# Tower of a small language model on one core: scores that add onto the ones left in their slot

## The chip, the cores and the metric

The kernel runs on one core of a Trainium2 chip. The metric is the device time of one execution in microseconds (us). Matmuls run on TensorE (PE in the rows; PEld is its weight load), elementwise work on VectorE (DVE), ScalarE (ACT) and GpSimd (POOL); SyncE (SP) issues most DMAs. TensorE writes its results to PSUM, which has eight banks of 512 fp32 columns; SBUF is the memory from which the engines read their operands.

## The reference

Two sequences of 1024 token ids go through an embedding with a short grouped convolution and a relu, then attention, then a mixture of experts with a fixed assignment of tokens. Nearly all of the time is attention:

```python
dots = jnp.einsum('bhqd,bhkd->bhqk', q, k) * scale      # 8 heads of 64, 1024 queries, 1024 keys
attn = jax.nn.softmax(dots, axis=-1)
out = jnp.einsum('bhqk,bhkd->bhqd', attn, v)
...
out = jnp.einsum('bne,ce->bnc', out, Wo)
```

Everything is fp32, and q and k are scaled so that softmax needs the maximum of each row.

## The kernel before

**Steps.** Eight steps (s, `STEPS`): two sequences, four pairs of heads each. A step has the queries in two halves of 512 and the keys in eight chunks of 128 (kc): 16 units. A unit is a PSUM slot of two banks, 128 keys by 2 x 512 queries (one bank for each head of the pair).

**A unit** (`scores`, L556). The operands are split in a rounded part and a rest, so that three products of reduced-precision matmuls, k_round q_round, k_round q_rest and k_rest q_round, give nearly fp32. Each product is a pair of matmuls, one for each head, with 64 rows and 512 columns, that run side by side. A fourth pair subtracts the maximum of each query (`minus_rows` times `max_rows_of`). ScalarE then takes exp of the slot into a tile of `probs` (L761), GpSimd adds the tiles for the denominators (L1160), and TensorE multiplies them with v into `acc_o` (L583), which has one bank for each half of the queries. In 44 of the 128 units (`FILLED`) the fourth pair is left out: ScalarE writes minus the maxima into the slot beforehand (`fill`, L813), from a plane that a DMA spreads over all partitions (`max_planes`), and the three products add onto it.

**Maxima.** A step ahead, TensorE makes rough scores of the next step with queries on the partitions (L509), VectorE reduces them (L961), joins the halves (L970) after each four chunks, and SP moves them by eight small DMAs to rows (`max_rows_of`, L386), a half (four chunks) at a time. Two maximum items stand in each part, as long as there are any; `AHEAD` is how many of them the prologue does.

**Order.** A step has eight parts of two units each. Every engine walks the same list of items and does its own share of each (`part_items`, L93), in program order: a maximum, two units, a maximum, then in part 0 k and q of the next step (twelve matmuls, L497; ScalarE copies the rounded parts, L770, VectorE subtracts for the rests, L956), in part 3 the denominators of the step before (L594), in step 7 the parts of the feed-forward (Wo, transposes, xa), a fill, and last the values (`pv`) of the two units of the part before. Every item that needs PSUM takes the next of three slots in turn (`n % SLOTS`), and TensorE waits until the item three places before has been read out (`release`).

**After the steps** the experts run in eight duos (L628, L639, L647). The prologue ahead of them makes the embedding, the normalised x, v (L476, through the two banks of `acc_o`), k and q of step 0, and the first maxima.

## Time and profile before

| | |
|---|---|
| Median of 3 runs | 408.73 us (408.3 to 408.97) |
| Profiled execution, its own time | 409.11 us |
| Its span | 407.2 us |
| TensorE matmuls busy | 395.0 us (97%) |
| VectorE busy | 224.5 us (55%) |
| ScalarE busy | 254.7 us (63%) |
| GpSimd busy | 292.7 us (72%) |
| Granted TensorE clock | 0.999 |

Times within the trace count from the start of the span. A matmul's length in the trace includes the time until its results have drained, so matmuls in a row overlap: what one costs is the distance from start to start.

### The profile page before, as it was taken

Reading aid. Unit: us, or ns where it says so; the run is one execution under the profiler, and the core shown is the slowest. Engines: PE = TensorE matmul, PEld = TensorE weight load, DVE = VectorE, ACT = ScalarE, POOL = GpSimd, SP = SyncE. Lnnn points to the kernel's source line nnn. Section 1 sums busy time; section 2 is a strip of 40 time slices with the busy share of each in tenths; the row PEclk is TensorE's granted clock in tenths of the full one; section 3 lists DMA queues with packets and bytes.
Section 4 is the critical chain, followed back from the end, with each engine's and each line's share of the span. In section 5 each row is a group of like instructions: output and inputs, shape, how many; then the busy total and the mean of one; then the engine's idle time right before and its main releaser. Section 6 shows DMA issues by size and latency. Waiting matters only on the chain.

```text
span 407.2 us, 6494 instructions
## 1 busy us (share of the span) xinstructions
PE 395.0 (97%) x2518; PEld 238.1 (58%) x2518; DVE 224.5 (55%) x304; ACT 254.7 (63%) x347; POOL 292.7 (72%) x145
## 2 busy tenths in 40 slices
PE   8898999999999999999999999999999989999996
PEld 8765554454555445544645555464558535489995
DVE  1798765565656555656665565657563700564322
ACT  1556566676667575767676575858573596436763
POOL 3062088969899989999998999899989487900011
PEclk9999999999999999999999999999999999999999
DMA  7000101011220121012103222240125014000001
GB/s 247 2 1 0 54 0 54 6 47 26 82 52 2 54 54 52 3 54 54 52 2 105 48 110 54 54 150 7 57 52 157 0 55 155 2 1 14 15 26 53
DMA packets 28507, 20.49 MB, mean 50 GB/s; under 512 B 21276, under 2 KB 23708, under 8 KB 28476
## 3 DMA queue, kind: packets, MB, share of 16 engines
q1 hardware_dynamic: 27900, 19.09, 17.3%
q10 hardware_dynamic: 576, 0.98, 0.7%
q8 instruction: 20, 0.33, 0.3%
q14 instruction: 11, 0.09, 0.1%
HBM read 18.77 MB, written 1.17 MB: 49 GB/s over the span
## 4 chain that ended last, share of the span: by engine, by line
PE 88%; DVE 4%; ACT 2%; DMA 2%; SPq 1%; issue 1%; POOL 0%; ACTq 0%; POOLq 0%
PE acc_o L583 27%; PE slot L571 24%; PE slot L509 9%; PE slot L497 6%; PE slot L518 4%; PE acc_o L639 4%; PE slot L628 4%; PE acc_o L476 2%; PE acc_o L436 2%; DVE half_maxes L961 2%; PE slot L594 2%; DMA max_plane<-rows_scratch 1%; SPq L386 1%; PE slot L451 1%; PE slot L534 1%; PE acc_o L451 1%
## 5 line engine op out<-in xcount | busy, mean ns | idle before, releaser
L961 DVE TENSOR_REDUCE half_maxes<-slot 128x2 f32<-128x1024 f32 x128 | 156.3, 1225 | 98.1 <-PE slot L509 97.9
L761 ACT ACTIVATE probs<-slot 128x1024 f32<-128x1024 f32 x128 | 124.7, 1024 | 82.2 <-PE slot L571 82.2
L583 PE MATMUL acc_o<-probs,v_all 128*64 128x512 f32 x512 | 123.7, 604 | 0.0
L1160 POOL TENSOR_TENSOR sums<-sums,probs 128x1024 f32<-128x1024 f32 x31 | 74.0, 2387 | 2.4 <-ACT probs L761 2.3
L1160 POOL TENSOR_TENSOR odd_sum<-odd_sum,probs 128x1024 f32<-128x1024 f32 x31 | 74.5, 2404 | 0.0
L1160 POOL TENSOR_TENSOR sums<-probs 128x1024 f32<-128x1024 f32 x16 | 37.9, 2368 | 44.0 <-ACT probs L761 44.0
L583 PEld LDWEIGHTS acc_o<-probs,v_all 128*64 128x64 f32 x512 | 31.2, 136 | 59.0 <-issue 39.7
L509 PE MATMUL slot<-k_round,q_round 64*128 64x512 f32 x256 | 56.9, 447 | 1.6 <-DVE half_maxes L961 1.3
L509 PEld LDWEIGHTS slot<-k_round,q_round 64*128 64x128 f32 x256 | 23.6, 183 | 57.0 <-issue 46.3
L571 PE MATMUL slot<-q_round,k_round 64*128 64x512 f32 x256 | 51.8, 400 | 1.7 <-ACT slot L819 0.8
L571 PE MATMUL slot<-q_round,k_rest 64*128 64x512 f32 x256 | 50.6, 390 | 0.0
L571 PE MATMUL slot<-q_rest,k_round 64*128 64x512 f32 x256 | 50.5, 389 | 0.0
L819 ACT ACTIVATE slot<-max_plane 128x1024 f32<-128x1024 f32 x44 | 45.2, 1028 | 2.8 <-DMA max_plane<-rows_scratch 1.7
L1166 POOL TENSOR_TENSOR sums<-sums,odd_sum 128x1024 f32<-128x1024 f32 x16 | 38.0, 2377 | 1.3
L1160 POOL TENSOR_TENSOR odd_sum<-probs 128x1024 f32<-128x1024 f32 x16 | 38.3, 2394 | 0.0
L1188 POOL TENSOR_TENSOR probs<-probs,residual 128x256 f32<-128x256 f32 x7 | 5.1, 726 | 43.2 <-ACT probs L870 43.2
L571 PE MATMUL slot<-max_rows_of,minus_rows 64*128 64x512 f32 x168 | 33.3, 389 | 0.0
L571 PEld LDWEIGHTS slot<-q_round,k_round 64*128 64x128 f32 x256 | 24.0, 184 | 11.3 <-issue 3.2
L571 PEld LDWEIGHTS slot<-q_round,k_rest 64*128 64x128 f32 x256 | 24.3, 184 | 5.4
L571 PEld LDWEIGHTS slot<-q_rest,k_round 64*128 64x128 f32 x256 | 24.2, 185 | 3.6
L863 ACT ACTIVATE probs<-slot,small 128x128 f32<-128x128 f32 x64 | 17.4, 383 | 11.4 <-PE slot L628 11.4
L571 PEld LDWEIGHTS slot<-max_rows_of,minus_rows 64*128 64x128 f32 x168 | 16.0, 184 | 3.3
(114 smaller groups left out, 423.1 us busy)
## 6 DMA issues: line engine op xcount, KB each, us to landing
max_plane<-rows_scratch SPq DMA_DIRECT2D x16, 512.0 KB, 3.6
inv_sb<-inv_scratch SPq DMA_DIRECT2D x14, 256.0 KB, 3.9
max_rows_of<-maxes SPq DMA_DIRECT2D x128, 0.5 KB, 2.0
v_all<-in_fc SPq DMA_DIRECT2D x4, 512.0 KB, 5.9
fc_late<-in_fc SPq DMA_DIRECT2D x4, 512.0 KB, 5.6
residual<-in_x SPq DMA_DIRECT2D x2, 512.0 KB, 5.9
out_h<-probs SPq DMA_DIRECT2D x8, 128.0 KB, 1.8
v_all<-in_w ACTq DMA_DIRECT2D x3, 256.0 KB, 7.4
```

The source lines that it names most:

```text
L497: last = pe.matmul(slot[:, half * BANK:(half + 1) * BANK], ws[:, w, v % PAIRS, :], xs[:, cols], start=(i == 0), stop=(i == 2))
L509: last = pe.matmul(slot[:, h * BANK:(h + 1) * BANK], q_round[p][head_rows(h), qc * CHUNK:(qc + 1) * CHUNK], k_round[p][head_rows(h), half ...
L518: last = pe.matmul(slot[:, j * C:(j + 1) * C], attn_out[:, b * PAIRS + r, j * CHUNK:(j + 1) * CHUNK], woT[:, r, :], start=(r == 0), stop=( ...
L571: last = pe.matmul(slot[:, h * BANK:(h + 1) * BANK], stationary, qs[head_rows(h), cols], start=(i == 0 and not ahead), stop=(i == len(term ...
L583: last = pe.matmul(acc_o[head_rows(h), cols], v_all[:, s, kc, head_rows(h)], probs[unit(s, kc, half) % TILES][:, h, :], start=(kc == 0), s ...
L628: last = pe.matmul(slot[:, i, r], expert(e)[:, 0, r, :], xaT[:, toks], start=True, stop=True)
L761: act.activation(probs[u % TILES][:, :, :].rearrange("p h n -> p (h n)"), slot[:, :], ACT.Exp, scale=SCALE).then_inc(exped, 1)
L819: act.activation(slots[n % SLOTS][:, :], max_planes[half][:, :], ACT.Copy, scale=-1.0).then_inc(filled_in, 1)
L863: act.activation(hidT[d % 2][:, i, r, :], slot[:, i, r], ACT.Gelu, bias=fc1_b_col[:, e * HC + r:e * HC + r + 1]).then_inc(hid_made, 1)
L961: dve.reduce_max(half_maxes[:, :, qc, keys], slot[:, :].rearrange("p (h n) -> p h n", h=2), AX.X).then_inc(maxed, 1)
L1160: pool.tensor_tensor(chain[:, :, :], first[:, :, :], probs[kc][:, :, :], ALU.add).then_inc(own, 1)
L1166: pool.tensor_tensor(even[:, :, :], even[:, :, :], odd_sum[:, :, :], ALU.add).then_inc(own, 1)
```

## The change

Within a half, the chunks of keys are taken in the order 0, 4, 1, 5, 2, 6, 3, 7 (`chunk_of`). Units with even kc use one slot, odd ones the other. Only the first unit in each slot (kc 0 and 1) computes its scores whole, with the pair for the maxima. Each later one adds (key chunk minus the chunk before it) times q onto the scores that are still in the slot, and has three pairs. `fill`, the planes and their DMAs are gone.

The third slot is for maxima alone (and in step 7 for transposes, xa and the last denominators). `acc_o`'s second bank becomes the place of k, q, the denominators and Wo; both halves' outputs go to its first bank in turn, but for the last half. k and q of the next step come in four pieces of 512 columns, between the first maximum and the units of parts 0, 1, 2 and 4. For each piece of k, ScalarE copies the first three chunks (`k_before`) and the rounded piece, and VectorE makes the rounded differences, their rests and the rest of the first chunk. `AHEAD` is 10 instead of 12, and the last four tiles of v come behind an earlier maximum.

The lists of items and places:

```diff
-AHEAD = 12
+AHEAD = 10
...
-                 ("max", *MAXES[7]): (8, 9, 10, 11), ("max", *MAXES[10]): (12, 13, 14, 15)}
+                 ("max", *MAXES[7]): (8, 9, 10, 11), ("max", *MAXES[9]): (12, 13, 14, 15)}
...
-FFN_ITEMS = {(STEPS - 1, 0): [("wo",)], (STEPS - 1, 3): [("nt",)], (STEPS - 1, 5): [("xa",)], (STEPS - 1, 6): [("last den", 0)]}
-
-
-PREFILLED = (2, 4, 6)
-UNFILLED = ((0, 2, 0), (STEPS - 1, 4, 0), (STEPS - 1, 4, 1))
+FFN_ITEMS = {(STEPS - 1, 0): [("wo", 1)], (STEPS - 1, 3): [("nt",)], (STEPS - 1, 5): [("xa",)], (STEPS - 1, 6): [("last den", 0)]}
+
+
+def chunk_of(kc):
+
+    return kc // 2 + kc % 2 * (KCH // 2)
...
-def beside_values(s, part):
-
-    items = []
-    if part == 0 and s + 1 < STEPS:
-        items += [("k", s + 1), ("q", s + 1)]
+def side_item(s, part):
+
+    if s == STEPS - 1 and part == 0:
+        return [("wo", 0)]
+    if s + 1 < STEPS and part in (0, 1, 2, 4):
+        return [{0: ("k", s + 1, 0), 1: ("k", s + 1, 1), 2: ("q", s + 1, 0), 4: ("q", s + 1, 1)}[part]]
+    return []
+
+
+def part_items(s, part):
+
+    maxes = [("max", *m) for m in MAXES[AHEAD + 2 * (s * PARTS + part):][:2]]
+    items = maxes[:1] + side_item(s, part)
+    items += [("exp", *u) for u in units_of(s, part)] + maxes[1:]
     if part == 3 and s > 0:
         items.append(("den", s - 1))
-    return items + FFN_ITEMS.get((s, part), [])
-
-
-def part_items(s, part):
-
-    maxes = [("max", *m) for m in MAXES[AHEAD + 2 * (s * PARTS + part):][:2]]
-    items = maxes[:1]
-    items += [("exp", *u) for u in units_of(s, part)] + maxes[1:]
-    beside = beside_values(s, part)
-    items += beside
-    if part % 4 < 3:
-        items.append(("fill", *units_of(s, part + 1)[0]))
+    items += FFN_ITEMS.get((s, part), [])
...
-FIRST_SLOT, LATE_SLOT, SUMS_SLOT = ((FIRST[-1] - 3 + i) % SLOTS for i in range(3))
+FIRST_SLOT, LATE_SLOT, SUMS_SLOT = range(SLOTS)
+SIDE = SLOTS
+
+
+def place(item):
+
+    if item[0] == "exp":
+        return item[2] % 2
+    return SUMS_SLOT if item[0] in ("max", "nt", "xa", "last den") else SIDE
+
+
+PLACES = [n % SLOTS for n in range(len(PROLOGUE))] + [place(item) for item in ALL_ITEMS[len(PROLOGUE):]]
+
+
+def item_before(n):
+
+    held = [m for m in range(n) if PLACES[m] == PLACES[n]]
+    return ALL_ITEMS[held[-1]] if held else None
...
-
-WHOLE_SLOT = ("exp", "max", "k", "q")
-FILLED = [item[1:] for n, item in enumerate(ALL_ITEMS)
-          if item[0] == "exp" and item[2] in PREFILLED and item[1:] not in UNFILLED and ALL_ITEMS[n - SLOTS][0] in WHOLE_SLOT]
...
-                return [sb(f"{name}{p}", [128, S], F32R, scope) for name in ("q_round", "q_rest", "k_round", "k_rest", "max_rows_of")]
+                steps = [sb(f"{name}{p}", [128, 2 * (KCH // 2 - 1) * CHUNK], F32R, scope) for name in ("k_step_round", "k_step_rest")]
+                return steps + [sb(f"k_rest{p}", [128, 2 * CHUNK], F32R, scope)] + [sb(f"{name}{p}", [128, S], F32R, scope) for name in ("q_round", "q_rest", "k_round", "max_rows_of")]
...
-            max_planes = [sb(f"max_plane{i}", [128, 2 * BANK], F32, att) for i in range(2)]
+            k_before = sb("k_before", [128, (KCH // 2 - 1) * CHUNK], F32, att)
```

Helpers of the places, the queue of SP and the preparation on TensorE:

```diff
+                    sp.wait_ge(split, 4 * STEPS)
                     load_experts(late[:2], fc_loaded[1])
             load_experts(late[2:], fc_loaded[1])
 
...
                     w = "qk".index(kind)
-                    for half in range(2):
+                    for half, piece in pieces_of(item, slot):
                         if v == 0 and kind == "k":
                             pe.wait_ge(x_rest, half + 1)
                         cols = slice(v // PAIRS * S + half * BANK, v // PAIRS * S + (half + 1) * BANK)
                         for i, (ws, xs) in enumerate(((wR, xR), (wL, xR), (wR, xL))):
-                            last = pe.matmul(slot[:, half * BANK:(half + 1) * BANK], ws[:, w, v % PAIRS, :], xs[:, cols],
...
@@ -503,19 +515,20 @@
                 else:
 
                     _, _, qc, half = item
-                    if qc == 0 and half == 0:
-                        pe.wait_ge(rounded, 2 * v + 2)
+                    if qc % GROUP == 0 and half == 0:
+                        pe.wait_ge(rounded, 4 * v + 3 + qc // GROUP)
```

Scores, values, and the wait ahead of each item:

```diff
                 if kc == 0 and half == 0:
-                    pe.wait_ge(split, 2 * s + 2)
-                terms = [(k_round[p], q_round[p]), (k_round[p], q_rest[p]), (k_rest[p], q_round[p])]
-                ahead = item[1:] in FILLED
-                if not ahead:
-                    terms.append((minus_rows, max_rows_of[p]))
-                for i, (ks, qs) in enumerate(terms):
+                    pe.wait_ge(split, 4 * s + 4)
+                if kc < 2:
+                    whole, rest = slice(chunk_of(kc) * CHUNK, (chunk_of(kc) + 1) * CHUNK), slice(kc * CHUNK, (kc + 1) * CHUNK)
+                    terms = [(k_round[p], whole, q_round[p]), (k_round[p], whole, q_rest[p]), (k_rest[p], rest, q_round[p]),
+                             (minus_rows, slice(0, CHUNK), max_rows_of[p])]
+                else:
+                    at = (chunk_of(kc) - kc % 2 - 1) * CHUNK
+                    own = slice(at, at + CHUNK)
+                    terms = [(k_step_round[p], own, q_round[p]), (k_step_round[p], own, q_rest[p]), (k_step_rest[p], own, q_round[p])]
+                for i, (ks, keys, qs) in enumerate(terms):
                     if i == 3 and kc == 0:
                         pe.wait_ge(rows_loaded, ROW_COUNT * (2 * s + half + 1))
                     for h in range(2):
-                        stationary = ks[head_rows(h), :] if i == 3 else ks[head_rows(h), keys]
-                        last = pe.matmul(slot[:, h * BANK:(h + 1) * BANK], stationary, qs[head_rows(h), cols],
-                                         start=(i == 0 and not ahead), stop=(i == len(terms) - 1), skip_group_check=ahead)
+                        last = pe.matmul(slot[:, h * BANK:(h + 1) * BANK], ks[head_rows(h), keys], qs[head_rows(h), cols],
+                                         start=(i == 0 and kc < 2), stop=(i == len(terms) - 1), skip_group_check=(kc > 1))
                 last.then_inc(filled, 1)
 
             def weigh_values(item):
 
                 _, s, kc, half = item
-                cols = slice(half * BANK, (half + 1) * BANK)
                 pe.wait_ge(exped, unit(s, kc, half) + 1)
-                if kc == 0 and s > 0:
-                    pe.wait_ge(o_copied, 2 * s - 1 + half)
+                if (s, kc, half) == (STEPS - 1, 0, 1):
+                    pe.wait_ge(den_copied, STEPS - 1)
+                elif kc == 0 and s + half > 0:
+                    pe.wait_ge(o_copied, 2 * s + half)
                 for h in range(2):
-                    last = pe.matmul(acc_o[head_rows(h), cols], v_all[:, s, kc, head_rows(h)],
+                    last = pe.matmul(out_bank(s, half)[head_rows(h), :], v_all[:, s, chunk_of(kc), head_rows(h)],
                                      probs[unit(s, kc, half) % TILES][:, h, :], start=(kc == 0), stop=(kc == KCH - 1))
...
-                    slot = slots[n % SLOTS]
-                    if item[0] == "exp" and item[1:] in FILLED:
-                        pe.wait_ge(filled_in, FILLED.index(item[1:]) + 1)
+                    slot, held = place_of(n), item_before(n)
+                    if held:
+                        pe.wait_ge(*release(held))
                     else:
-                        pe.wait_ge(*release(ALL_ITEMS[n - SLOTS]))
+                        pe.wait_ge(v_sb, NCH)
```

ScalarE's and VectorE's share of k and q:

```diff
-                    act.copy((q_round if kind == "q" else k_round)[item[1] % 2][:, :], slot[:, :]).then_inc(rounded, 1)
+                    whole = (q_round if kind == "q" else k_round)[item[1] % 2]
+                    for half, piece in pieces_of(item, slot):
+                        if kind == "k":
+                            if 2 * item[1] + half > 0:
+                                act.wait_ge(step_split, 2 * item[1] + half)
+                            act.copy(k_before[:, :], piece[:, 0:BANK - CHUNK]).then_inc(k_copied, 1)
+                        act.copy(whole[:, half * BANK:(half + 1) * BANK], piece).then_inc(rounded, 1)
...
-            def fill(unit_item):
-
-                _, s, kc, half = unit_item
-                n = ALL_ITEMS.index(("exp", s, kc, half))
-                act.wait_ge(*release(ALL_ITEMS[n - SLOTS]))
-                act.wait_ge(plane_loaded, 16 * (2 * s + half) + 16)
-                act.activation(slots[n % SLOTS][:, :], max_planes[half][:, :], ACT.Copy, scale=-1.0).then_inc(filled_in, 1)
...
-                elif kind in "qk":
-                    v = item[1]
-                    whole, rest = (q_round, q_rest) if kind == "q" else (k_round, k_rest)
-                    dve.wait_ge(rounded, 2 * v + (1 if kind == "k" else 2))
-                    dve.tensor_tensor(rest[v % 2][:, :], slot[:, :], whole[v % 2][:, :].bitcast(F32),
-                                      ALU.subtract).then_inc(split, 1)
+                elif kind == "q":
+                    p = item[1] % 2
+                    for half, piece in pieces_of(item, slot):
+                        cols = slice(half * BANK, (half + 1) * BANK)
+                        dve.wait_ge(rounded, 4 * item[1] + 3 + half)
+                        dve.tensor_tensor(q_rest[p][:, cols], piece, q_round[p][:, cols].bitcast(F32), ALU.subtract).then_inc(split, 1)
+                elif kind == "k":
+                    for half, piece in pieces_of(item, slot):
+                        key_steps(item[1], half, piece)
...
+            def key_steps(v, half, piece):
+
+                p, count = v % 2, 2 * v + half + 1
+                width = BANK - CHUNK
+                own, first = slice(half * width, (half + 1) * width), slice(half * CHUNK, (half + 1) * CHUNK)
+                later, before = piece[:, CHUNK:BANK], k_before[:, :]
+                dve.wait_ge(k_copied, count)
+                dve.wait_ge(rounded, 4 * v + half + 1)
+                dve.tensor_tensor(k_step_round[p][:, own], later, before, ALU.subtract).then_inc(step_rounded, 1)
+                dve.wait_ge(step_rounded, count)
+                dve.tensor_tensor(later, later, k_step_round[p][:, own].bitcast(F32), ALU.subtract).then_inc(step_partly, 1)
+                dve.wait_ge(step_partly, count)
+                dve.tensor_tensor(k_step_rest[p][:, own], later, before, ALU.subtract).then_inc(step_split, 1)
+                dve.tensor_tensor(k_rest[p][:, first], piece[:, 0:CHUNK], k_round[p][:, half * BANK:half * BANK + CHUNK].bitcast(F32),
+                                  ALU.subtract).then_inc(split, 1)
```

The rest of the diff follows from these: Wo's two halves are items of their own, and the waits on counts of `split`, `rounded` and `o_copied` are counted in pieces.

## Rows read from the trace of the kernel before

**Rows 1.** Windows, one step: us; busy of PE, PEld, DVE, ACT, POOL; clock; DMA:

```profile
118.50:156.20 37.70, 37.70 (x236) 19.73 (x234) 22.56 (x21) 25.37 (x27) 35.26 (x16) 1.00 0.18 44
```

**Rows 2.** The page's chain of waits, shares of the span by engine:

```profile
PE 88%; DVE 4%; ACT 2%; DMA 2%; SPq 1%; issue 1%; POOL 0%; ACTq 0%; POOLq 0%
```

**Rows 3.** Timeline, start and length in us: step 1's first maximum:

```profile
80.77 0.50 PE L509 MATMUL slot<-k_round,q_round 64*128 64x512 f32 x2
```

**Rows 4.** Timeline of one part, start and length in us:

```profile
152.04 0.50 PE L509 MATMUL slot<-k_round,q_round 64*128 64x512 f32 x2
...
152.38 0.39 PE L571 MATMUL slot<-q_round,k_round 64*128 64x512 f32 x2
...
152.58 1.23 DVE L961 TENSOR_REDUCE half_maxes<-slot 128x2 f32<-128x1024 f32 x1 [1.07 <-PE slot L509]
...
153.28 1.95 ACT L761 ACTIVATE probs<-slot 128x1024 f32<-128x1024 f32 x2 [1.14 <-PE slot L571]
...
154.00 0.40 PE L509 MATMUL slot<-k_round,q_round 64*128 64x512 f32 x2
...
154.32 1.94 PE L583 MATMUL acc_o<-probs,v_all 128*64 128x512 f32 x8
...
156.19 0.50 PE L509 MATMUL slot<-k_round,q_round 64*128 64x512 f32 x2
```

**Rows 5.** The page's costliest groups: count, busy us, mean ns:

```profile
L819 ACT ACTIVATE slot<-max_plane 128x1024 f32<-128x1024 f32 x44 | 45.2, 1028 | 2.8 <-DMA max_plane<-rows_scratch 1.7
...
L571 PE MATMUL slot<-max_rows_of,minus_rows 64*128 64x512 f32 x168 | 33.3, 389 | 0.0
```

**Rows 6.** Chain in order of time: start, length, the block of k and q:

```profile
158.75 3.00 PE slot L497 x12
```

**Rows 7.** Timeline, the last matmul of values before the step and the next maxima:

```profile
42.19 0.40 PE L476 MATMUL acc_o<-wvL,xR 128*128 128x512 f32 x1
...
42.52 0.73 PE L509 MATMUL slot<-k_round,q_round 64*128 64x512 f32 x4
```

**Rows 8.** Timeline of a maximum that waited for its slot:

```profile
52.42 0.19 PEld L509 LDWEIGHTS slot<-k_round,q_round 64*128 64x128 f32 x2 [0.37 <-DVE half_maxes L961]
52.42 0.51 PE L509 MATMUL slot<-k_round,q_round 64*128 64x512 f32 x2
...
52.86 0.20 PEld L583 LDWEIGHTS acc_o<-probs,v_all 128*64 128x64 f32 x4 [0.25 <-issue]
```

**Rows 9.** Groups by shape: count, busy us, mean ns:

```profile
L956 DVE TENSOR_TENSOR k_rest<-slot,k_round 128x1024 fp32r<-128x1024 f32 x8 | 9.8, 1224 | 10.1 <-ACT k_round L770 10.1
...
L827 ACT COPY attn_out<-acc_o 128x512 f32<-128x512 f32 x14 | 8.2, 584 | 6.8 <-PE acc_o L583 6.7
...
L1079 DVE TENSOR_TENSOR probs<-acc_o,next_b_row 128x256 f32<-128x256 f32 x8 | 3.4, 423 | 12.7 <-PE acc_o L647 12.7
```

**Rows 10.** Chain and SP's timeline around the rows of maxima:

```profile
54.23 0.18 DVE maxes L970
...
58.84 2.02 DMA max_rows_of<-maxes
...
147.61 5.86 SPq L386 DMA_DIRECT2D max_rows_of<-maxes  x8
```

**Rows 11.** Timeline of the prologue:

```profile
22.12 1.02 ACT L770 CAST k_round<-slot 128x1024 fp32r<-128x1024 f32 x1 [1.79 <-PE slot L497]
...
25.83 2.33 DVE L961 TENSOR_REDUCE half_maxes<-slot 128x2 f32<-128x1024 f32 x2
```

**Rows 12.** Timeline of step 7:

```profile
309.51 7.41 PE L518 MATMUL slot<-woT,attn_out 128*128 128x128 f32 x64
...
321.76 0.50 PE L509 MATMUL slot<-k_round,q_round 64*128 64x512 f32 x2 [0.94 <-DVE half_maxes L961]
...
324.02 1.85 DVE L1023 SCALAR_TENSOR_TENSOR shift<-mv,rstd 128x8 f32<-128x8 f32 x2
...
332.22 1.09 PE L525 MATMUL slot<-ident,normed 128*128 128x128 f32 x8 [1.11 <-ACT probs L761]
```

More of the change, by code:

```diff
@@ L545, in ffn_item @@
                     pe.wait_ge(wo_loaded, 16)
-                    wo_half(0, 0, slot)
-                    last = wo_half(0, 1, slot)
+                    last = wo_half(0, item[1], slot)
                 elif kind == "nt":
@@ L750, in act_item @@
             def act_item(item, n):
-                kind, slot = item[0], slots[n % SLOTS]
+                kind, slot = item[0], place_of(n)
                 if kind == "exp":
@@ L946, in dve_item @@
             def dve_item(item, n):
-                kind, slot = item[0], slots[n % SLOTS]
+                kind, slot = item[0], place_of(n)
                 if kind == "features":
@@ L972, in dve_item @@
                     dve.wait_ge(filled, n + 1)
-                    for half in range(2):
-                        add_and_stats(0, half, slot)
+                    add_and_stats(0, item[1], slot)
                 elif kind == "last den":
```

60 lines of the change are left out of this document (27 added, 33 removed).

## The prediction

> **What bounds the kernel now.** I read the stretches by step first: between 118.5 and 156.2 us TensorE is busy in all 37.70 us, GpSimd in 35.26, ScalarE in 25.37, VectorE in 22.56, and the granted clock is full [rows 1]. The chain of waits says the same: PE 88%, DVE 4% [rows 2]. That is a step: the first maximum of step 1 stands at 80.77 [rows 3], that of step 2 at 118.5, and so on in periods of 37.70. So only what TensorE issues, or newly waits for, counts there; what ScalarE is spared counts nothing.
>
> The sum is made against the profiled execution (span 407.2, time 409.11), which is 0.38 above the median of 408.73. I carry differences over to the median. A measurement of this kernel can tell some 0.2%, 0.8 us, from no change.
>
> **One part of a step, from the timeline** [rows 4]. The first maximum item starts at 152.04, the scores at 152.38, so 0.34 for it. From there seven pairs of matmuls follow until 154.00, 0.23 each, so six are 1.38. Second maximum to values 0.32 (154.00 to 154.32), values 1.87 (to 156.19). A part with six score pairs is 0.34 + 1.38 + 0.32 + 1.87 = 3.91, with eight 4.37.
>
> **What goes.** The term of the maxima stands in 168 matmuls [rows 5], 84 pairs; afterwards only kc 0 and 1 have it, two units in each of 16 halves, 32 pairs. 52 x 0.23 = 12.0 us leave TensorE, 1.5 a step. The 44 fills of 1.03 us [rows 5] leave ScalarE, which idles anyway: nothing. The planes' DMAs go: nothing, except that SP's queue is freer.
>
> **k and q in pieces, on TensorE.** Before, twelve matmuls cost 3.00 in one block [rows 6]. Now four blocks of three lie between a maximum and the scores. A switch from a full to a half tile takes 0.33 instead of 0.23 (42.19 to 42.52 [rows 7]), so a block costs 3 x 0.23 + 2 x 0.10 = 0.89, four 3.56. Bounds for the switches: 0 to 0.2 each block beyond the 0.69; I take the row's.
>
> Step without waits: 8 x 3.91 + 4 x 0.23 + 3.56 + 1.0 (denominators: 37.70 - 8 x 3.91 - 10.5 x 0.23 - 3.00) = 36.8. That would be 0.9 less than 37.70. Now the waits.
>
> **First new wait: one slot for maxima.** Maxima alternated over three slots; now the second waits until VectorE has reduced the first. The reduce starts 0.54 after the first's matmuls and takes 1.23 [rows 4]: free at 1.77 + 0.04, where the second would start at 0.34 + 1.38 = 1.72. And a pair started by a wait exposes its weight load, which starts with it: 52.42 to 52.86 is 0.44 against 0.32 [rows 8]. So 0.09 + 0.11 = 0.20 in parts with six pairs and no block: 3, 5, 6, 7. In the others the block or the two more pairs cover it. 0.8 a step. Bounds: 0 (if the wait is met just in time) and 0.3.
> The Trainium skill ("TensorE: Matmul & The Clock Gate", Step-by-step) says that TensorE pulls weight loads ahead of matmuls in flight. By that the 0.11 would vanish at each wait; the rows show the load starting with its matmul where a wait stands ahead, so I price it. The difference would be about 0.5 a step, 3 us in all.
>
> **Second new wait: the key differences on VectorE.** A k block is followed on ScalarE by two copies (384 and 512 columns) and on VectorE by three subtractions of 384 and one of 128, in program order ahead of the second maximum's reduce. Durations: 1024 columns 1.224 and 256 columns 0.423 [rows 9], so 384 is 0.56 and 128 is 0.29; ScalarE's 512 is 0.584 [rows 9], 384 about 0.47. From the part's start: block at 0.34 + 0.09 = 0.43, scores 0.79 later, its last matmul ends 1.28; copies until 2.30; subtractions 2.34 to 4.27 (they wait for each other, 0.02 each); reduce until 5.40; TensorE may write the maxima slot at 5.43. A part with a k block and eight pairs (part 0) would be 0.43 + 0.79 + 1.84 + 0.32 + 1.87 = 5.25, with six (part 1) 4.79. Waits 0.18 and 0.64, 0.8 a step. Queued behind: the next maximum, and behind it in TensorE's order everything. Bounds: 0.3 less each (0.35 a step) to 0.3 more each (1.4).
> The q blocks have one subtraction of 0.7 and end in time.
> The Trainium skill ("PSUM — Partial Sum Buffer", Engine vs sequencer instructions) calls VectorE's queue strict FIFO. By it the reduce, whose data are there at 3.5, must wait for the subtractions; if the ready one could pass, the 0.8 a step would be nothing.
>
> **Third: rows of maxima come later.** With AHEAD 10 instead of 12 the fourth chunk's maximum of the next step falls in part 6 instead of 5. The join of maxima ends 3.79 into part 6 (second maximum at 1.81, reduce from 2.36 to 3.59, join 0.2); from a join's end (54.41) to the last row's landing (58.84 + 2.02 = 60.86) it takes 6.45 [rows 10]: 10.26 after part 6 began. The max term of kc 0 stands at 2 x 4.11 + 1.91 = 10.13. Wait 0.13 + 0.11 = 0.24, of which 0.18 is inside the wait above: 0.06 a step. But eight issues took 5.86 instead of 5.0 once [rows 10], so up to 0.9 a step; the long one stood beside the loads of inv_sb, which will be over by then, so I take the short one. The other half has 1.7 us more.
>
> **Step after:** part 0 5.49, part 1 5.43, part 2 4.79, part 3 4.11 + 1.0, part 4 5.25, parts 5 to 7 12.33: 38.4. Against 37.70 that is +0.7, and for steps 1 to 6 +4.4.
>
> **Third score slot gone.** Scores of a slot need its exp, one part before. ScalarE starts 0.04 after the last matmul's end and needs 1.95 for two [rows 4]; even in part 0 it is done at 4.4, and the slot is wanted at 5.4 + 1.2. No wait. One bank for the outputs: the copy (0.6) ends 2 us ahead of the next use. No wait.
>
> **Prologue.** The k item of step 0 is whole, two pieces, and k_before is one buffer: ScalarE's second k_before waits for the first piece's third subtraction, and q's copies stand behind it. From ScalarE's start at 22.12 [rows 11]: copies until 23.08, three subtractions until 24.83; second pair of copies until 25.83, q until 26.85; subtractions of k until 27.75, of q until 29.0, two small reciprocals; the first reduce of maxima at 29.2, which before started at 25.83 [rows 11]. All later items hang on VectorE there (the features and half of the values need its rests). That is +3.3, bounds 1.5 (if slack takes half) and 3.6.
>
> **Step 0.** Without the prologue's 3.3 its first maximum stands at 42.29, one pair ahead of the one at 42.52 [rows 7]. Part 0 has no values yet, so the k chain shows whole, and its block waits 0.3 for the last copy of v: 5.73. Parts 1 to 7 as above, without denominators: 5.43 + 4.79 + 4.11 + 5.25 + 12.33. It ends at 79.9, where before it was 80.77 [rows 3]: -0.8.
>
> **Step 7.** No k and q. Nine max pairs fewer (by FILLED 13, now 4): -2.1. Two more maxima in part 2: +0.7. The wait of 0.94 in part 1 (321.76 [rows 12]), made by both halves of Wo at once on VectorE, becomes 0.2: -0.8. Wo (7.41 in one) in two blocks: +0.2. The transposes' wait of 1.11 for a score slot [rows 12] goes: -1.1. But the new maxima of part 2 stand behind VectorE's shift, which ends at 325.87 [rows 12]; the first of them is reduced only then, until 327.1. The second would have started at 324.8 (321.76 - 0.94, + 0.32 + 1.87 for the next part's start, + 1.81): +2.3. Sum -0.8. From the experts on nothing changes.
>
> **Sum:** 3.3 - 0.8 + 4.4 - 0.8 = +6.1. Profiled 415.2; median 408.73 + 6.1 = **414.8**.
>
> **Rivals.**
> - *The saved matmuls win* (other side). VectorE has only 22.56 of 37.70 us of work [rows 1], and if its short subtractions run closer than I extend from the long ones (the chain of part 1 at most 4.8 long), the second wait is gone: -4.9; with the first wait's exposed load hidden too, -2.6, and half the prologue, -1.7: 414.8 - 9.2 = 405.6. It decides at a chain of 4.8 in a k part. Against it: the rows of 256 and 1024 columns fix 384 within 0.05. Chance 0.14.
> - *No change*: the same, in part, 408 to 409.5. Chance 0.06.
> - *The rows of maxima are late in every step* (0.8 more each, 6 times): 414.8 + 4.8 = 419.6. For: the moment is missed by 0.13 already, so every slowing counts in full. Against: no other DMA stands near. Chance 0.15.
> - *ScalarE becomes the bound, since two score slots tie each unit to its exp*: a wait of 0.3 in each of 64 parts would give 434. The margins above are over 1 us. Chance 0.04. GpSimd, with 35.3 busy a step, would only bind if the step fell below that: it caps the gain of the first rival, no more.
> - *It doesn't do what it says*: the adds onto old scores cost extra on TensorE. The matmuls onto filled slots before are of the same kind and pitch (the three pairs from 152.38 [rows 4] go onto a filled slot, 0.23 each). Chance 0.01; each 0.1 us more in a unit would be +10.
> - Forecast: 0.60, its own range 412 to 418.
>
> The range takes in rival three mostly and reaches down to the no-change cases: 408 to 420. Slower: 0.60 + 0.15 + 0.04 + 0.01 = 0.80, same 0.06, faster 0.14.
>
> **What the profile after would show.** The group of score matmuls on max_rows_of with 64 instead of 168; steps of 38.4 from the start of one first maximum to the next's; the second maximum's load idle for VectorE's half_maxes in parts 3, 5, 6, 7, some 0.1 to 0.2 each; the first maxima of parts 1 and 2 waiting 0.2 and 0.6 for the same; VectorE busy without a gap from the first subtraction to the reduce's end; max rows landing within 0.3 of their term; the first reduce at 29.2; step 0's first maximum at 45.6. I am wrong if the step is below 37.7 or the first reduce starts before 27.

## The result, and the profile after

The changed kernel takes 424.7 us (median of 4 runs, 424.25 to 425.62), the kernel before 408.85 beside it: ratio 1.040, interval 1.0387 to 1.0420. The forecast was 414.8, its range 408 to 420: the direction was right, the size was not. The profiled execution took 424.74 us with a span of 422.9, so its span is 15.7 longer than before; 6.1 of that was forecast. 9.6 have to be found.

First the page: its chain of waits, by engine, and its busiest groups. TensorE's share of the chain falls from 88% [rows 2] to 77%, VectorE's rises from 4% to 13%: the engine that had little part in the end now has a real one.

```profile
PE 402.4 (95%) x2414; PEld 227.1 (54%) x2414; DVE 245.5 (58%) x368; ACT 218.4 (52%) x335; POOL 292.2 (69%) x145
...
PE 77%; DVE 13%; ACT 3%; DMA 2%; issue 2%; SPq 1%; DVEq 0%; ACTq 0%
```

Then the windows of one step (us; busy PE, PEld, DVE, ACT, POOL; clock; DMA): 39.27 where before stood 37.70 [rows 1] and the forecast was 38.4.

```profile
95.61:134.88 39.27, 38.68 (x222) 18.20 (x220) 25.07 (x31) 20.32 (x25) 35.27 (x16) 1.00 0.09 15
```

**A block of q, part 4 of step 5.** TensorE's timeline: start, length. A switch is a change of tile size between two matmuls, here from 64x128 (maxima, scores) to 128x128 (the block) and back. From the maximum (225.70) to the block it is 0.43, from the block's first to its second matmul 0.34, from its last to the first scores 0.33, from these to the second pair 0.34. Each would be 0.23 without a switch but the first, which would be 0.34. The block costs (226.13 - 225.70) + (227.38 - 226.13) - 0.34 - 0.23 = 1.11. I had put 0.89.

```profile
225.70 0.50 PE L521 MATMUL slot<-k_round,q_round 64*128 64x512 f32 x2
226.13 0.50 PE L510 MATMUL acc_o<-xR,wR 128*128 128x512 f32 x1
226.47 0.40 PE L510 MATMUL acc_o<-xR,wL 128*128 128x512 f32 x1
226.71 0.40 PE L510 MATMUL acc_o<-xL,wR 128*128 128x512 f32 x1
227.04 0.50 PE L586 MATMUL slot<-q_round,k_round 64*128 64x512 f32 x2
227.38 0.40 PE L586 MATMUL slot<-q_rest,k_round 64*128 64x512 f32 x2
```

The weight loads show half of the price. Behind a switch the load starts with its own matmul (226.13, 227.04), and the next load 0.11 later; elsewhere a load starts with the matmul before its own. The 0.34 behind each switch goes with that. What the 0.10 ahead of it is, no run separates.

```profile
226.13 0.19 PEld L510 LDWEIGHTS acc_o<-xR,wR 128*128 128x128 f32 x1 [0.25 <-issue]
226.24 0.19 PEld L510 LDWEIGHTS acc_o<-xR,wL 128*128 128x128 f32 x1
...
227.04 0.19 PEld L586 LDWEIGHTS slot<-q_round,k_round 64*128 64x128 f32 x2 [0.37 <-issue]
```

**A part with neither block nor term, part 5.** The second maximum starts 1.82 behind the first and the values 0.44 later, as forecast (0.2 over 1.72 and 0.32).

```profile
231.20 0.50 PE L521 MATMUL slot<-k_round,q_round 64*128 64x512 f32 x2
...
233.02 0.50 PE L521 MATMUL slot<-k_round,q_round 64*128 64x512 f32 x2
233.46 1.94 PE L599 MATMUL acc_o<-probs,v_all 128*64 128x512 f32 x8
235.32 0.49 PE L521 MATMUL slot<-k_round,q_round 64*128 64x512 f32 x2
```

**The chain of VectorE in a k part.** Part 1 starts at 209.91. The last row is TensorE's: it waits 0.54 for the reduce, and the part is 215.57 - 209.91 = 5.66 long (forecast 5.43). The four subtractions run without a gap, at the lengths taken. Those that wait for the one before start 0.59 to 0.60 behind it; the last one and the reduce wait for none, and start 0.48 behind a length of 0.56 and 0.20 behind one of 0.28.

```profile
212.43 0.56 DVE L1008 TENSOR_TENSOR k_step_round<-acc_o,k_before 128x384 fp32r<-128x384 f32 x1 [0.75 <-ACT k_round L792]
213.02 0.57 DVE L1010 TENSOR_TENSOR acc_o<-acc_o,k_step_round 128x384 f32<-128x384 f32 x1
213.62 0.56 DVE L1012 TENSOR_TENSOR k_step_rest<-acc_o,k_before 128x384 fp32r<-128x384 f32 x1
214.10 0.28 DVE L1013 TENSOR_TENSOR k_rest<-acc_o,k_round 128x128 fp32r<-128x128 f32 x1
214.30 1.22 DVE L976 TENSOR_REDUCE half_maxes<-slot 128x2 f32<-128x1024 f32 x1
...
215.57 0.50 PE L521 MATMUL slot<-k_round,q_round 64*128 64x512 f32 x2 [0.54 <-DVE half_maxes L976]
```

**Something not forecast.** The windows of three places where TensorE idles, each with the window behind it. At 21 to 29, 50 to 53 and 336 to 342 it is busy 4.59 of 8, 1.03 of 3 and 4.20 of 6 us; behind each the granted clock is 0.60, 0.57 and 0.66 on average. In the kernel before it was 1.00 from 7.4 to 406.7 us, but no wait of TensorE there is longer than 1.11 behind the first 2 us.

```profile
21.00:29.00 8.00, 4.59 (x20) 2.87 (x19) 6.93 (x24) 4.25 (x10) 2.43 (x2) 1.00 0.00 1
29.00:33.30 4.30, 4.30 (x14) 3.03 (x13) 2.93 (x4) 1.76 (x3) 4.22 (x4) 0.60 0.04 0
50.00:53.00 3.00, 1.03 (x6) 0.67 (x5) 2.37 (x5) 0.89 (x1) 0.00 (x0) 1.00 0.01 3
53.00:57.00 4.00, 4.00 (x18) 2.36 (x18) 2.88 (x6) 2.60 (x4) 0.79 (x1) 0.57 0.00 0
...
336.00:342.00 6.00, 4.20 (x26) 1.95 (x24) 3.98 (x5) 5.94 (x8) 5.12 (x3) 1.00 0.01 3
342.00:347.00 5.00, 4.47 (x14) 1.56 (x16) 1.87 (x3) 3.49 (x9) 4.25 (x2) 0.66 0.03 0
```

**Where the 15.7 lie.** Step 1's first maximum stands at 85.51 (before 80.77 [rows 3]): +4.7. Step 7's stands at 322.08 (before 306.97), so steps 1 to 6 are +10.4. From there to the end it is 100.8 against 100.2: +0.6. The forecast had +2.5, +4.4 and -0.8. One more thing stands in step 3: the last of the eight rows of maxima lands 3.06 behind its issue, where the last row of 13 of the other 15 halves takes 2.02 to 2.04, and the term of the maxima waits for it. It comes 1.20 behind the matmul before it instead of 0.23, so the late row costs about 0.95.

```profile
164.05 3.06 DMA max_rows_of<-maxes
...
167.16 0.50 PE L586 MATMUL slot<-max_rows_of,minus_rows 64*128 64x512 f32 x2 [0.82 <-DMA max_rows_of<-maxes]
```

### The profile page after: what moved, and what is told of

The parts are those of the page before. It is cut to its first block, busy times and chain, and to the rows that moved or that the text cites. A ratio compares the mean times of both kernels' runs of the same rounds, so it can differ in the third digit from the quotient of the medians.

```text
span 422.9 us, 6274 instructions
## 1 busy us (share of the span) xinstructions
PE 402.4 (95%) x2414; PEld 227.1 (54%) x2414; DVE 245.5 (58%) x368; ACT 218.4 (52%) x335; POOL 292.2 (69%) x145
## 3 DMA queue, kind: packets, MB, share of 16 engines
HBM read 10.38 MB, written 1.11 MB: 27 GB/s over the span
## 4 chain that ended last, share of the span: by engine, by line
PE 77%; DVE 13%; ACT 3%; DMA 2%; issue 2%; SPq 1%; DVEq 0%; ACTq 0%
PE acc_o L599 23%; PE slot L586 19%; PE slot L521 10%; PE acc_o L510 6%; DVE half_maxes L976 4%; PE acc_o L655 3%; PE slot L644 3%; PE acc_o L489 3%; PE acc_o L531 2%; DVE k_step_round L1008 2%; PE slot L531 2%; DVE k_step_rest L1012 2%; ACT k_round L792 2%; PE acc_o L610 2%; DMA residual<-in_x 2%
## 5 line engine op out<-in xcount | busy, mean ns | idle before, releaser
L521 PE MATMUL slot<-k_round,q_round 64*128 64x512 f32 x256 | 60.5, 471 | 11.7 <-DVE half_maxes L976 8.0
L586 PE MATMUL slot<-q_round,k_step_round 64*128 64x512 f32 x192 | 40.7, 418 | 0.0
L586 PE MATMUL slot<-q_round,k_step_rest 64*128 64x512 f32 x192 | 38.5, 394 | 0.0
L586 PE MATMUL slot<-q_rest,k_step_round 64*128 64x512 f32 x192 | 38.4, 395 | 0.0
L792 ACT CAST q_round<-acc_o 128x512 fp32r<-128x512 f32 x14 | 8.2, 587 | 37.2 <-PE acc_o L510 37.2
L586 PEld LDWEIGHTS slot<-q_round,k_step_round 64*128 64x128 f32 x192 | 18.5, 188 | 11.4 <-issue 8.5
L586 PEld LDWEIGHTS slot<-q_round,k_step_rest 64*128 64x128 f32 x192 | 18.5, 187 | 4.2
L586 PEld LDWEIGHTS slot<-q_rest,k_step_round 64*128 64x128 f32 x192 | 18.7, 189 | 3.4
L791 ACT COPY k_before<-acc_o 128x384 f32<-128x384 f32 x14 | 6.7, 480 | 23.0 <-PE acc_o L510 23.0
L841 ACT COPY attn_out<-acc_o 128x512 f32<-128x512 f32 x14 | 8.2, 586 | 18.9 <-PE acc_o L599 18.9
```

Source lines behind the costliest of these rows:

```text
L521: last = pe.matmul(slot[:, h * BANK:(h + 1) * BANK], q_round[p][head_rows(h), qc * CHUNK:(qc + 1) * CHUNK], k_round[p][head_rows(h), half ...
L586: last = pe.matmul(slot[:, h * BANK:(h + 1) * BANK], ks[head_rows(h), keys], qs[head_rows(h), cols], start=(i == 0 and kc < 2), stop=(i == ...
L792: act.copy(whole[:, half * BANK:(half + 1) * BANK], piece).then_inc(rounded, 1)
```

## The experiments

All times are medians, and differences are to the changed kernel's 424.7. Each kernel ran beside the kernel before, whose median was 408.55 to 408.79 (408.85 beside the changed kernel). Theory: three terms beyond the forecast, (a) both sides of each switch of tile size, (b) TensorE at its lower clock behind idle stretches, (c) the one late row; and the forecast's two waits for VectorE. The periods below are from the start of one maximum's reduce to that 16 later, in the middle of the run; for the changed kernel 39.30.

**Half-row blocks.**
```
+ rows = slice(0, 64 if v > 0 else 128)
- pe.matmul(piece, ws[:, w, ...], xs[:, cols])
+ pe.matmul(piece, ws[rows, w, ...], xs[rows, cols])
```


> Against the changed kernel: from step 1 on the key and query projections use only rows 0 to 63 of both operands, so they are half tiles as the scores are (half of the input features are left out of these products; instructions and columns are the same). Theory (the switch between full and half tiles costs 0.4 us more a block than forecast, .34 at the block's first matmul and .11 at the first pair of scores after it): parts 2 and 4 of a step 0.4 us shorter, parts 0 and 1 by 0.2 us or nothing, as VectorE's chain holds them: -0.8 to -1.2 us a step, -6 to -8 us in all. Rival (the excess is not the switch): 0.


Measured: 418.6, so -6.1; the period is 38.05, so -1.25 a step. Between the reduces' starts parts 2 and 4 lost 0.44 each, part 0 0.11 and part 1 0.22, as VectorE's chain holds those two. The excess is the switch. Six such periods are -7.5; on the other side the mean granted clock from 20 to 60 us is 0.83 instead of 0.91 in this profile, and in every step the term of the maxima now comes 0.3 late for its row.

**Shorter reduces.**
```
- slot.rearrange("p (h n) -> p h n", h=2)
+ slot.rearrange("p (h n) -> p h n", h=2)[:, :, 0:448 if v > 0 else BANK]
```


> Against the changed kernel: from step 1 on the reduces of scores read 448 of 512 columns a head (an eighth of the keys is left out of the maxima), so each is 0.13 us shorter. Theory (VectorE's turnover of the two score slots is on TensorE's path, as forecast): the wait of 0.2 us of the parts with two maxima and no block goes, and parts 0 and 1 lose 0.13 us each: about -0.9 us a step, -6 to -7 us in all. Rival (those waits are not what sets the part's length): 0 to -1 us.


Measured: 418.6, so -6.1; the period is 38.45 to 38.49, so six periods are -5, and its profile has no fall of the clock in step 7 (1.6, below). In a part with six pairs the second maximum now starts 1.72 behind the first (228.62 to 230.34), but the values 0.41 later: the load behind it is still exposed.

**One more subtraction a half.**
```
+ dve.tensor_tensor(k_step_rest[p][:, own], later, before, ALU.subtract)   # again below
```


> Against the changed kernel: from step 1 on VectorE makes one more key difference of 384 columns a half (0.56 us and a gap of 0.05 us, twice a step). Theory (VectorE's chain ends last in parts 0 and 1 of each step): +0.6 us in each of the two parts, +1.2 us a step, +8 us in all. Rival (TensorE's own matmuls and switches set these parts): under +2 us.


Measured: 429.8, so +5.1; the period is 40.17, +0.87 to 0.90. Parts 0 and 1 are 6.10 and 6.11 long instead of 5.63 and 5.65, so 0.47 more each, and not the 0.6 expected. That is all that the extra subtraction adds to the chain: the one behind it doesn't wait for it and starts 0.47 later, though it is 0.56 long.

```profile
217.04 0.56 DVE L1009 TENSOR_TENSOR k_step_rest<-acc_o,k_before 128x384 fp32r<-128x384 f32 x1 [0.74 <-ACT k_round L792]
217.51 0.55 DVE L1010 TENSOR_TENSOR k_step_round<-acc_o,k_before 128x384 fp32r<-128x384 f32 x1
```

So VectorE's chain sets the end of parts 0 and 1, without slack.

**Remainder of k after the reduce.**
```
- dve.tensor_tensor(k_rest[p][:, first], piece[:, 0:CHUNK], ...)    # ahead of the reduce
+ pending.append(...)                                              # issued behind it, v > 0
```


> Against the changed kernel: in steps 1 to 7 VectorE makes the 128-column remainder of the keys after the next pair's reduce instead of ahead of it. Theory (the chain copy, four key steps, reduce on VectorE binds parts 0 and 1 of each step): the reduce starts 0.28 us earlier in both parts, up to 0.2 us of it each on the path (as much as the part's waits hold): -0.4 us a step, about -2.9 us in all. Rival (the excess of parts 0 and 1 is the switch between full and half tiles): 0.


Measured: 421.2, so -3.5; the period is 38.90, -0.4 a step, as expected. Six such periods are -2.4. The profile, whose clock doesn't fall in step 7 (1.6, below), and whose late row costs 0.2 more, is 3.7 shorter.

Here are windows of one step of these four, in the order above; TensorE has 222 matmuls in each. In the second and third VectorE's busy time is 22.95 and 26.02 instead of 25.07, and the period moves with it. In the first and fourth it is 25.07 as in the changed kernel: there the period is shorter by the tile size of the blocks and by the order of VectorE's work.

```profile
219.76:257.81 38.05, 37.12 (x222) 18.37 (x220) 25.07 (x29) 20.31 (x25) 35.20 (x16) 1.00 0.18 43
```
```profile
218.70:257.19 38.49, 38.06 (x222) 18.18 (x220) 22.95 (x29) 20.33 (x25) 35.26 (x16) 1.00 0.16 42
```
```profile
226.19:266.36 40.17, 38.63 (x222) 18.06 (x220) 26.02 (x32) 20.33 (x25) 35.22 (x16) 1.00 0.17 41
```
```profile
219.88:258.78 38.90, 38.55 (x222) 18.08 (x220) 25.07 (x29) 20.32 (x25) 35.30 (x16) 1.00 0.16 42
```

**VectorE made light**, to see the step without its waits.
```
- dve.reduce_max(..., slot[:, :].rearrange("p (h n) -> p h n", h=2), ...)
+ dve.reduce_max(..., slot[:, :].rearrange("p (h n) -> p h n", h=2)[:, :, 0:256 if v > 0 else BANK], ...)
...
- dve.tensor_tensor(later, later, k_step_round[p][:, own].bitcast(F32), ALU.subtract)
+ few = width if v == 0 else 16
+ dve.tensor_tensor(later[:, 0:few], later[:, 0:few], k_step_round[p][:, own][:, 0:few].bitcast(F32), ALU.subtract)
```


> Against the changed kernel: from step 1 on VectorE's reduces read half of the keys and one of the three key subtractions is cut to 16 columns (left out: half of the keys in the maxima, most of the rounding error of the stepped keys). No wait for VectorE should be left. Theory (the step of 39.27 us is 36.8 forecast without waits, + 0.22 in each of four blocks for the switches between full and half tiles, + 1.6 of waits for VectorE): the period of a step becomes 37.7 us, that of the kernel before, and the time falls by some 11 us. Rival (there is an excess somewhere else in the step): the period stays over 38.2 us.


Measured: 411.95, so -12.7; the period is 37.65. That closes the step: 36.8 + 0.9 for switches + 1.6 of waits = 39.3. It says more: even with no wait for VectorE the changed step would be as long as the old one (37.70 [rows 1]). The switches ate what the saved matmuls gave: four blocks at 0.42 are 1.7 a step where the one block before paid 0.23, so +1.45 against -1.5.

```profile
213.90:251.55 37.65, 37.65 (x222) 18.30 (x220) 15.78 (x30) 20.30 (x25) 35.23 (x16) 1.00 0.17 43
```

**The clock: dummy matmuls in the idle stretches.**
```
+ keep_warm(14, slots[2])    # prologue, ahead of the first maximum
+ keep_warm(8, bank(6))      # step 0, ahead of part 1's first maximum
+ keep_warm(9, bank(7))      # step 7, ahead of part 2's second maximum
```


> Against the changed kernel: dummy matmuls (identity by identity, never read) fill TensorE's three idle stretches: 14 in the prologue ahead of the first pair of scores, 8 ahead of step 0's first maximum of part 1, 9 in step 7 ahead of the second maximum of part 2. Theory (the granted clock falls to the 1.2 GHz level after each of these idle stretches, and that is a term of its own): the granted clock stays near 1.00 at 29 to 33, 53 to 57 and 342 to 347 us, and the time falls by 1.3 + 1.4 + 1.5 = 4.2 us. Rival (the stretches at the lower level only fill time that VectorE's waits would have taken anyway): the clock stays up and the time moves by less than 1 us.


Measured: 422.25, so -2.45 of 4.2. The granted clock is 1.00 in all three windows, step 7's part from the Wo block to the end is 1.6 shorter, and the seventeenth reduce (at 64.10 in the changed kernel) starts at 62.42. From ScalarE's first key copy to that reduce it is 40.75 instead of 42.93, so prologue and step 0 brought 2.2. But step 1 then waits for its rows of maxima, and the term comes 1.45 late (first line from the chain of waits):

```profile
84.17 3.57 DMA max_rows_of<-maxes
...
87.79 0.50 PE L586 MATMUL slot<-max_rows_of,minus_rows 64*128 64x512 f32 x2 [1.30 <-DMA max_rows_of<-maxes]
```

The wait is the row's own: it took 3.57, and with the usual 2.0 it would have been there at 86.2, in time. One term in step 0 and one in step 4 are 0.25 and 0.6 late too, and the late row of step 3 isn't there. So the three places of the clock brought 2.2 and 1.6, the late rows +1.45, +0.25, +0.6 and -0.95, together -2.45.

A cleaner pair is the same wait of TensorE in step 7 in kernels that don't differ there. First the changed kernel: 2.33 of wait, then values of 3.37 us for eight matmuls. Then the one with the late remainder: a wait of 2.30, and the values take 1.94.

```profile
342.53 0.50 PE L521 MATMUL slot<-k_round,q_round 64*128 64x512 f32 x2 [2.33 <-DVE half_maxes L976]
342.96 3.37 PE L599 MATMUL acc_o<-probs,v_all 128*64 128x512 f32 x8
```
```profile
340.48 0.49 PE L521 MATMUL slot<-k_round,q_round 64*128 64x512 f32 x2 [2.30 <-DVE half_maxes L978]
340.90 1.94 PE L599 MATMUL acc_o<-probs,v_all 128*64 128x512 f32 x8
```

From that window on, changed kernel first: clock 0.66 against 1.00, with 3.50 and 3.58 us of 5.8 busy ahead of it.

```profile
336.70:342.50 5.80, 3.50 (x22) 1.56 (x18) 4.32 (x5) 5.74 (x8) 5.45 (x3) 1.00 0.01 3
342.50:347.50 5.00, 4.97 (x19) 1.94 (x21) 1.40 (x2) 3.02 (x9) 3.75 (x2) 0.66 0.05 0
```
```profile
334.60:340.40 5.80, 3.58 (x22) 1.56 (x19) 4.35 (x5) 5.74 (x8) 5.44 (x3) 1.00 0.01 3
340.40:345.40 5.00, 4.92 (x31) 1.92 (x31) 1.42 (x3) 4.68 (x10) 4.38 (x3) 1.00 0.05 0
```

From the last reduce's start to the end it is 79.8 in the changed kernel, 79.9 in the one with the second buffer and 79.7 in that with half-row blocks, all three with the fall, and 78.2 in the four without it (short reduces, one more subtraction, late remainder, block ahead). So a fall there costs 1.6 us, and it comes in some executions and not in others.

**Maxima 11 items ahead.**
```
-AHEAD = 10
+AHEAD = 11
```


> Against the changed kernel: the maxima run 11 instead of 10 items ahead of the values, so that rows of maxima are loaded half a part earlier, and step 7's part 2 holds only one maximum. Theory (late rows and the double maximum of step 7 cost what the trace shows): 0.9 us less where step 2's row was waited for, 2.3 us of waiting and some 1.5 us of lower clock less in step 7, about -4 us in all; the first matmul of maxima rows waits 0.1 us or less in every step. Rival (the maximum that leaves part 2 waits as long where it goes): less than 1 us less.


Measured: 422.05, so -2.65 of 4. The profiled execution took 420.92, so -3.8; the three slower runs of five (422.05 to 422.66) had a lower granted clock on average, 0.987 against 0.990 and 0.991. All periods of steps 2 to 6 are 39.23 to 39.27: the late row (c) is gone. From the Wo block to the end it is 97.7 instead of 100.4; the wait of 2.33 and the fall are gone, but the transposes now wait 0.98 for ScalarE, and scores wait 0.4 for a slot.

**A second buffer in the prologue.**
```
- act.copy(k_before[:, :], ...)
+ act.copy((den_sb if 2 * item[1] + half == 1 else k_before)[:, 0:BANK - CHUNK], ...)
```


> Against the changed kernel: the second half of step 0's key copy goes into a buffer of its own (den_sb, not used yet then), so that ScalarE doesn't wait for VectorE's key steps in the prologue. Theory (that wait of 1.9 us stands on the prologue's path): the first reduce of the scores starts about 1 us earlier and the time falls by 1 us; by 2.3 us if TensorE's shorter idle time also keeps the granted clock up at 29 us. Rival (VectorE's own four key steps a half set the end): under 0.3 us.


Measured: 423.1, so -1.6. In the profiled execution the first reduce starts at 28.36 against 28.31, no earlier; but there the whole prologue ran 1.06 later (ScalarE's first key copy at 22.23 against 21.17). From that copy to the reduce it is 6.13 instead of 7.14, the 1 us expected. The first fall stays; it only starts earlier, at 28.1 instead of 29.3 us. The one at 53 did not come in this profile: from the thirteenth to the seventeenth reduce it is 10.65 instead of 11.54, so that fall cost 0.9.

**The block beside the values.** Before the change, TensorE's timeline shows where the block of twelve stood: behind the second maximum and ahead of the values, whose tiles are 128x64: all rows, half of the columns. From maximum to values it is 3.31 there against 0.32 without a block: 2.99, or 12 x 0.23 and 0.23 for switches. The change moved the blocks between two groups of 64-row tiles, where they pay 0.42.

```profile
158.37 0.39 PE L509 MATMUL slot<-k_round,q_round 64*128 64x512 f32 x2
158.74 0.50 PE L497 MATMUL slot<-xR,wR 128*128 128x512 f32 x1
...
161.37 0.39 PE L497 MATMUL slot<-xL,wR 128*128 128x512 f32 x1
161.68 1.94 PE L583 MATMUL acc_o<-probs,v_all 128*64 128x512 f32 x8
```
```
-    items = maxes[:1] + side_item(s, part)
+    items = side_item(s, part) + maxes[:1]      # steps 0 to 6; VectorE keeps the old order
```


> Against the changed kernel: TensorE issues each block of k or q ahead of its part's first maximum, so right behind the full tiles of the values, instead of between two groups of half tiles; VectorE still reduces the first maximum ahead of the key differences. Theory (both switches of a block cost 0.2 us each, and here none is added; the chain of VectorE starts behind the same maximum and gives the next maximum the block's time): parts 2 and 4 become 0.4 us shorter, parts 0 and 1 0.4 us each, a step 37.6 to 38.0 instead of 39.27, some -9 to -11 us in all. Rival (a full tile beside the values' half-wide tiles pays the switch as well, or VectorE's chain holds parts 0 and 1): under -5 us.


Measured: 417.2, so -7.5, between the two; the period is 38.27, -1.0. The block costs 0.90 (238.34 to 239.24), so 0.21 of switches. I had expected none. The rows show why there is one: every change of tile size costs 0.21, from the values' 128x64 to the block's 128x128 too (238.34 to 238.68 is 0.34). Between two groups of 64-row tiles a block adds two changes; behind the values it adds one, since from values to maximum there is one anyway.

```profile
236.47 1.94 PE L599 MATMUL acc_o<-probs,v_all 128*64 128x512 f32 x8
238.34 0.50 PE L510 MATMUL acc_o<-xR,wR 128*128 128x512 f32 x1
238.68 0.39 PE L510 MATMUL acc_o<-xR,wL 128*128 128x512 f32 x1
238.91 0.40 PE L510 MATMUL acc_o<-xL,wR 128*128 128x512 f32 x1
239.24 0.51 PE L521 MATMUL slot<-k_round,q_round 64*128 64x512 f32 x2
239.58 0.40 PE L586 MATMUL slot<-q_round,k_round 64*128 64x512 f32 x2
```

The four blocks save 0.85 a step. The second wait is gone from parts 0 and 1, but the first wait, which a block used to cover in parts 1 and 2, now stands there too (the maxima at 206.49 and 208.31 are 1.82 apart, the values come 0.44 later), and in each of steps 1, 2 and 4 to 6 the term of the maxima comes about 0.1 late for its row.

**The edits together**, without and with dummy matmuls. The first kernel has the block ahead, `AHEAD = 11` and the second buffer; the second adds `keep_warm(14, slots[2])` and `keep_warm(8, bank(6))`, in the prologue and step 0 only.

> The kernel of the block ahead of the maximum, with two more edits together: maxima 11 items ahead, and a buffer of its own for the second key copy of the prologue. Theory (the savings are of separate places and add up: -9 to -11, -2.6 and -1.0 us): 410 to 412 us. Rival (the maxima that are made earlier meet the longer VectorE chain): no better than the block ahead alone.

> The kernel before it, with the dummy matmuls in the prologue and ahead of step 0's first maximum of part 1 too. Theory (the granted clock's fall at 29 and 53 us is a cost beside the others): 1 to 2.5 us less than without them, 408 to 411 us, about the kernel before the change. Rival (what they bring is lost where step 1 waits for its rows of maxima): the same time as without them.


Measured: 412.8 without (409.56 to 413.37), 411.3 with; the savings nearly add up, the period is 38.04. The lowest of the first, 409.56, is its profiled execution, and there the clock is 1.00 throughout, although TensorE is busy 1.02 of the 3 us from 24 to 27. With the dummies the spread is smaller (410.88 to 412.05), but they cost where no fall would have come: from ScalarE's first key copy to the seventeenth reduce it is 38.31 against 36.62. Against the kernel before, the one with dummies is 1.0057, interval 1.0038 to 1.0075: the repaired change is still slower, by about 2.5 us, near the six steps' 6 x (38.04 - 37.67) = 2.2. No version here beats the kernel before.

## Why the prediction was wrong

Two terms carry the miss: the price of a switch, sized at half of what it costs (6.2 us), and TensorE's clock behind idle stretches, put at nothing (3.8 us).

- *Step without waits, 36.8.* This is the step that failed. I took 0.10 for each switch from one row (42.19 to 42.52 [rows 7]), the pitch across the switch. The pitch after it is 0.34 too; it stood in [rows 4], in the 0.34 of each first maximum, and I had built it into the part and not into the block. Four blocks, 0.22 more each: 0.9 a step, 5.3 in steps 1 to 6. My bounds for a block's switches, 0 to 0.2, don't hold the 0.42 that it paid. The half-row blocks gave back 1.25 a step, and the light VectorE left 37.65. I also did not ask between which tiles the block was moved. The Trainium skill ("TensorEngine Tiling (Array Packing)", Key Properties) warns that a change of the tiling mode drains TensorE, with no price. The rows here agree that a change costs, 0.10 ahead and 0.11 behind each; that it is a drain they don't show.
- *First wait, 0.8 a step.* Right to the hundredth in its row (1.82 and 0.44). The shorter reduce showed half of it, the light VectorE all.
- *Second wait, 0.8 a step.* Right as a net: parts 0 and 1 are 5.64 and 5.66, forecast 5.49 and 5.43; the chain ends at 5.61, forecast 5.40, because the block in front of it is 0.2 longer. The forecast's own lengths put end to end give 5.58 and not 5.40. It came out because an instruction that doesn't wait for the one before starts ahead of that one's end, as shown above; no reason stood there for it.
- *Rows of maxima, 0.06 a step.* Right in five of the six steps; in step 3 the row is 0.95 late. The rival of late rows (0.8 in every step) was wrong as a rule, but this is no accident of one execution: in all but one of the nine profiles with ten maxima ahead the last row for step 3 took 2.7 to 3.3, and the term came 0.4 to 1.4 late; in the ninth, with dummies, that happened in steps 1 and 4. As forecast, no other load of SyncE is under way then, so why these rows are slow stays open. That the rows are met without slack, as the rival said, shows with the half-row blocks and the block ahead: there the term is 0.3 and 0.1 late in nearly every step.
- *Third score slot, outputs' bank: nothing.* No such wait in steps 1 to 6.
- *Prologue, +3.3.* From ScalarE's first key copy to the first reduce it is 7.14, forecast 7.08. What I left out is what TensorE does after idling there: twelve matmuls of values take 4.54 (28.73 to 33.27) at the lower clock, and 3.24 in the profile of the edits together without dummies, which had no fall (27.90 to 31.14).
- *Step 0, -0.8.* Came out at +1.1 (4.7 less the prologue's 3.3 and its fall's 1.3, plus the earlier start's 0.95): 0.9 for the fall at 53, 0.9 for its four blocks.
- *Step 7, -0.8.* All terms as forecast, the wait 2.33 for 2.3; then 1.6 for the fall behind it: +0.6.
- Together: switches 6.2 (seven steps), late row 0.9, clock 3.8 (1.3, 0.9, 1.6), less 0.95 for the earlier start: 9.95, where 9.6 was to be found. 0.2 of the difference is my own sum (six steps of +0.7 are +4.2, not +4.4); 0.15 stays open. Each fall's price is from a pair of profiles with and without it; the dummies brought the same 3.8 at these three places, and 2.45 in all, as other rows came late.
- Both signs of being wrong that I named, a step below 37.7 and a first reduce before 27, lay on the fast side. The step was 39.27 and the reduce at 28.31, so neither came, and the forecast was wrong all the same.
- The Trainium skill on weight loads ("TensorE: Matmul & The Clock Gate", Step-by-step): it speaks of loads pulled ahead of matmuls in flight, and by it I let 0.11 vanish at each wait. Behind a wait the trace shows no load pulled ahead, 0.44 from the row at 233.02 to the next; no matmul is in flight there, so this doesn't contradict the page, and my reading of it as a rival went too far.
- The Trainium skill on VectorE's strict FIFO ("PSUM — Partial Sum Buffer", Engine vs sequencer instructions): the trace agrees. The reduce issued behind k_rest started at 214.30 with its data long there, and 0.28 of work moved behind it took 0.2 off each of the two parts.

## What to carry to other kernels

Price a moved piece of work by its neighbours, and count the changes of tile size that it adds: each cost 0.21 here, half ahead of it and half behind. Between two groups of 64-row tiles a block paid 0.42, behind the values 0.21. Saved matmuls on the busiest engine are worth only what is left after the waits and switches that pay for them; make one run with the new waits taken out before repairing anything. And where a forecast has TensorE idle for a while, price the work behind it at the lower of its two clock levels as well.

## What the runs showed of the hardware

- TensorE's granted clock fell to its lower level (pitch of a 512-column matmul 0.43 instead of 0.23, so 1.2 instead of 2.4 GHz) behind waits of 1.6, 1.1 and 0.7 us close together, of 2.0, and of 2.3. With the same wait to a few hundredths it did not fall in other executions: behind the 2.3 in step 7 it fell in three profiles of seven; behind 1.75 and 0.70 in the prologue it fell with the second buffer alone and not with the edits together. So its cost is a chance, and it spreads the runs.
- The start of the whole program moves by up to 1 us from one execution to the next (the first key copy at 21.17 and 22.23 in kernels that are the same up to there). Places in two profiles are to be compared from a common event, not from zero.
- A 384-column subtraction of VectorE is 0.56 long, but one behind it that doesn't wait for it starts after 0.47, and one that waits for it after 0.59 (217.04, 217.51 and 218.10 in the kernel with one more subtraction).
- Half-row blocks ran side by side with one head's scores, as this timeline of the half-row kernel shows, and a block of three still cost 0.69 (3 x 0.23): no gain from that, but no switch either.

```profile
224.67 0.39 PE L511 MATMUL acc_o<-xR,wR 64*128 64x512 f32 x1
224.68 0.50 PE L587 MATMUL slot<-q_round,k_round 64*128 64x512 f32 x1
224.90 0.39 PE L511 MATMUL acc_o<-xR,wL 64*128 64x512 f32 x1
```
